# A four-batch decoder layer on one core: more stages in halves, two batches of masks spread by TensorE, memsets later, a new hand-written order

## The reference, cut to what matters

```
x = x + attn(layernorm(x))            # softmax(-gamma * |yi - yj|^2) @ y, 512 x 512 a batch
x = x + xattn(layernorm(x), ctx)      # q, k, v, 16 heads; scores = q.k/sqrt(8) + slope*(i-j)
x = x + ffn(layernorm(x))             # 8 experts, the 2 with the largest logits are summed

logits = einsum('bsh,eh->bse', hidden_states, router_w) + router_b
_, top_k_indices = top_k(softmax(logits), 2)
mask = one_hot(top_k_indices, E).sum(axis=-2)
out = einsum('bse,ehd,bsd->bsh', mask, expert_w, hidden_states) + einsum('bse,eh->bsh', mask, expert_b)
```

## Time and profile before

| | |
|---|---|
| median of 3 runs | 208.95 us (208.78 to 220.65) |
| the profiled execution, device time | 208.65 us |
| its span | 206.9 us |
| PE, share of the span with a matmul | 91% |
| DVE | 70% |
| ACT | 50% |
| POOL | 35% |
| mean granted TensorE clock | 0.984 of full speed |

### The profile page before, as it was taken

One profiled execution on the slowest core, in us unless ns is written; L12 is line 12 of the kernel. 1 busy time (PEld: TensorE's weight loads), 2 busy tenths in 40 slices (PEclk: granted clock), 3 DMA queues, 4 the chain that ended last, 5 costly groups with the idle time before them and its releaser, 6 DMA issues. The chain is left out here.

```text
span 206.9 us, 4043 instructions
## 1 busy us (share of the span) xinstructions
PE 188.4 (91%) x1418; PEld 119.8 (58%) x1427; DVE 144.2 (70%) x395; ACT 104.1 (50%) x204; POOL 72.3 (35%) x122
## 2 busy tenths in 40 slices
PE   7999999998999999799988876799998999698894
PEld 2454589744475432546585456753397854398674
DVE  2844969799999999195249999787188712736662
ACT  2037989739625888799850300178613638400100
POOL 6986014166500000024504289205906000793000
PEclk9999999999999999999999999999999789979999
DMA  4910073582710000640479047023000024000002
GB/s 126 355 15 2 21 196 113 153 194 91 187 46 21 0 0 12 175 121 3 143 141 302 22 154 150 22 73 133 28 36 0 8 82 182 0 0 3 2 0 101
DMA packets 12972, 17.66 MB, mean 85 GB/s; under 512 B 1332, under 2 KB 10548, under 8 KB 12256
## 3 DMA queue, kind: packets, MB, share of 16 engines
q1 hardware_dynamic: 12952, 17.41, 29.4%
HBM read 11.02 MB, written 6.38 MB: 84 GB/s over the span
## 5 line engine op out<-in xcount | busy, mean ns | idle before, releaser
L1103 DVE TENSOR_REDUCE nm<-bank 128x3 f32<-128x462 f32 (+1 forms) x88 | 48.3, 612 | 5.3 <-PE bank L1337 5.0
L926 ACT ACTIVATE pt<-bank 128x512 f32<-128x512 f32 x80 | 41.9, 615 | 8.7 <-PE bank L1375 8.1
L1472 PE MATMUL bank<-ewT,ym 128*128 128x128 f32 x256 | 35.1, 291 | 0.0
L1472 PEld LDWEIGHTS bank<-ewT,ym 128*128 128x128 f32 x256 | 32.7, 205 | 0.8 <-issue 0.6
L813 POOL TENSOR_TENSOR ym<-mask_all,y3T 128x512 f32<-128x512 bf16 x24 | 27.2, 1168 | 13.4 <-DMA mask_all<-e_scratch 13.4
L1337 PE MATMUL bank<-ks,qs 99*128 99x308 bf16 (+1 forms) x171 | 26.0, 263 | 1.3 <-DVE nm L1103 1.2
L796 POOL TENSOR_SCALAR ve<-mv 128x4 f32<-128x4 f32 (+1 forms) x5 | 1.0, 196 | 67.8 <-DVE mv L987 67.8
L1337 PEld LDWEIGHTS bank<-ks,qs 99*128 99x128 bf16 x171 | 13.4, 98 | 15.2 <-DVE nm L1103 6.2
L1375 PE MATMUL bank<-qs,ks 105*128 105x512 bf16 (+1 forms) x80 | 20.6, 342 | 0.6 <-DMA qs<-m_scratch 0.6
L1214 PE MATMUL bank<-idle 128*128 128x512 bf16 x60 | 16.4, 426 | 1.7 <-DVE idle L978 1.5
L1404 PE MATMUL bank<-pt,vm 128*32 128x512 f32 (+1 forms) x160 | 17.7, 518 | 0.0
(11 more groups left out here) (143 smaller groups left out, 271.4 us busy)
## 6 DMA issues: line engine op xcount, KB each, us to landing
mask_all<-e_scratch SPq DMA_DIRECT2D x3, 1024.0 KB, 5.0
ks<-k_scratch SPq DMA_DIRECT2D x4, 480.0 KB, 4.2
q_scratch<-qpart SPq DMA_DIRECT2D x3, 384.0 KB, 2.5
qs<-q_scratch SPq DMA_DIRECT2D x3, 384.0 KB, 4.8
xs<-in_x_dram SPq DMA_DIRECT2D x4, 256.0 KB, 4.0
k_scratch<-mask_all SPq DMA_DIRECT2D x4, 240.0 KB, 2.4
q_scratch<-qpart SPq DMA_DIRECT2D x3, 256.0 KB, 2.1
qs<-q_scratch SPq DMA_DIRECT2D x3, 256.0 KB, 5.3
```

What stands on the lines that cost most here:

```text
L926: nc.scalar.activation(pt[:, n % RING, :], at("scores", b, i)[:, :], ACT.Exp).then_inc(exps, 1)
L1103: v.tensor_reduce(nm[b][:, n:n + heads], at("maxima", b, g)[:, 0:heads * J].rearrange("p (s j) -> p s j", s=heads), AX.X, ALU.max, negate= ...
L1472: last = mm(at("experts", b, p)[:, tile(t)], ym[:, e, tile(t)], ewT[:, e, :], start=False, stop=(e == E - 1), skip_group_check=True)
```

## The change

The configuration, and what the table of dummy matmuls becomes:

```diff
-PARTS2 = (2, 1, 1, 1)
-PARTS3 = (1, 1, 1, 2)
+PARTS2 = (2, 2, 2, 2)
+PARTS3 = (1, 1, 2, 2)
...
-SPREAD = (3,)
+SPREAD = (2, 3)
...
 WARM = {
-    "y1T:0.0": 43, "kp:0.0": 2, "sqT:0.0": 1, "maxima:1.0": 3, "divide:0.1": 2, "aoT:0.0": 1, "maxima:2.0": 9,
-    "y2T:3.0": 2, "route:1.0": 1, "y3T:3.0": 1, "spread:3.0": 1,
+    "y1T:0.0": 28, "sqT:0.0": 4, "probs:1.1": 3, "maxima:0.0": 5, "y2T:3.0": 22, "query:3.0": 2,
+    "maxima:2.0": 1,
 }
```

All five texts of `ORDER` and the eight of `TURNS` are rewritten. One line of POOL's and one of DVE's:

```diff
     "gpsimd": """
-        weights:0.0 setup:0.0 gamma:0.0 zeros:0.0 rstd1:0.0 rstd1:1.0 squares:0.0 bias:0.0 y1g:1.0 squares:1.0
+        setup:0.0 gamma:0.0 rstd1:0.0 squares:0.0 bias:0.0 rstd1:1.0 squares:1.0 y1g:1.0 zeros:0.0 weights:0.0
...
     "vector": """
...
+        y2:0.0 key_values:0.1 rowmax:1.0 key_values:0.2 key_values:0.3 gather:0.1 split:0.0 y1:2.0 y2:0.1
+        keys:0.1 gather:1.0 split:0.1 dist:2.0 dist:2.1 y2:1.0 gather:1.1 y1:3.0 dist:2.2 dist:2.3 y2:1.1
```

```diff
-        q_out = [[sem(f"q_out{i}_{k}") for k in range(3 * PARTS2[i])] for i in range(B)]
+        q_out = [[sem(f"q_out{i}_{k}") for k in range(3 * max(PARTS2[i::2]))] for i in range(2)] * 2
...
-                pool.wait_ge(gamma_ready, 2)
...
-                pool.wait_ge(rstd1_ready, g_ + 1)
-
             def squares(g_, _):
 
                 m = members(g_)
+                pool.wait_ge(rstd1_ready, g_ + 1)
+                pool.wait_ge(gamma_ready, 2)
...
-                    act.wait_ge(e_in, ONE * b)
+                    act.wait_ge(e_in, ONE * sum(i not in SPREAD for i in range(b)))
...
             def select(b, k):
-                p, e = k // (E // 2), k % (E // 2) * 2
+                per = PARTS3[b]
+                p, e = k * per // E, k * per % E
...
-                dve.wait_ge(spread_ps, k + 1)
+                dve.wait_ge(spread_ps, E * SPREAD.index(b) + k + 1)
```

More of the change, by code:

```diff
@@ L141 @@
-        values:1.2 scores:1.19 self:3.0 values:1.3 values:1.4 mask:0.0 divide:1.0 divide:1.1 self:3.1 probs:3.2
-        aoT:1.0 wo:1.0 probs:3.3 self:3.2 self:3.3 maxima:2.0 maxima:2.1 maxima:2.2 maxima:2.3 maxima:2.4
-        maxima:2.5 maxima:2.6 y2T:3.0 maxima:2.7 y3T:1.0 maxima:2.8 maxima:2.9 query:3.0 maxima:2.10
-        maxima:2.11 maxima:2.12 maxima:2.13 maxima:2.14 maxima:2.15 maxima:2.16 maxima:2.17 experts:0.0
-        maxima:2.18 maxima:2.19 maxima:2.20 maxima:2.21 route:1.0 experts:0.1 experts:0.2 experts:0.3 mT:2.0
@@ L161 @@
-        spread:3.5 spread:3.6 experts:3.8 spread:3.7 experts:3.9 experts:3.10 experts:3.11 experts:3.12
-        experts:3.13 experts:3.14 experts:3.15
+        start:0.0 y1T:0.0 sqT:0.0 dist:0.0 dist:0.1 dist:0.2 keys:0.0 dist:0.3 y1T:1.0 keys:0.1 sqT:1.0
+        key_values:0.0 sqT:2.0 probs:0.0 dist:1.0 probs:0.1 self:0.0 probs:0.2 self:0.1 dist:1.1 dist:1.2
+        dist:1.3 probs:0.3 self:0.2 y2T:0.0 self:0.3 query:0.0 probs:1.0 probs:1.1 self:1.0 y1T:2.0 probs:1.2
+        y2T:0.1 sqT:3.0 query:0.1 self:1.1 dist:2.0 probs:1.3 dist:2.1 self:1.2 self:1.3 dist:2.2 y2T:1.0
@@ new lines @@
+        self:3.0 values:0.4 divide:0.0 scores:1.0 scores:1.1 divide:0.1 scores:1.2 probs:3.3 scores:1.3
+        scores:1.4 aoT:0.0 scores:1.5 self:3.1 scores:1.6 wo:0.0 scores:1.7 scores:1.8 scores:1.9 scores:1.10
+        scores:1.11 values:1.0 scores:1.12 scores:1.13 scores:1.14 values:1.1 scores:1.15 scores:1.16
+        scores:1.17 scores:1.18 values:1.2 values:1.3 y2T:2.0 scores:1.19 divide:1.0 query:2.0 values:1.4
+        y2T:2.1 y3T:0.0 divide:1.1 query:2.1 route:0.0 aoT:1.0 self:3.2 wo:1.0 self:3.3 mask:0.0 y2T:3.0
@@ new lines @@
+    """,
+    """
+        dist:0.1 sqT:2.0 query:0.1 y2T:1.0 y1T:3.0 maxima:0.7 probs:2.0 probs:2.1 maxima:0.19 maxima:1.2
+        maxima:1.6 maxima:1.11 scores:0.2 maxima:1.17 scores:0.9 scores:0.12 scores:0.16 self:3.0 maxima:2.2
+        maxima:2.8 maxima:2.14 maxima:2.20 maxima:3.1 pv:2.0 scores:2.11 scores:2.14 scores:2.17 maxima:3.18
+        experts:1.0 experts:2.0 experts:3.1
+    """,
+    """
+        dist:0.2 dist:1.0 y2T:0.0 self:1.0 dist:2.3 maxima:0.9 dist:3.1 maxima:0.21 maxima:1.4 maxima:1.9
+        probs:3.2 scores:0.1 maxima:1.16 scores:0.8 scores:0.11 mT:1.0 pv:0.1 scores:1.2 scores:1.5 scores:1.9
+        scores:1.13 scores:1.18 y3T:0.0 mask:0.0 y2T:3.1 maxima:2.6 maxima:2.13 mask:1.0 scores:2.3 scores:2.7
+        maxima:3.9 divide:2.0 maxima:3.19 scores:3.0 mT:3.1 pv:3.0 scores:3.11 scores:3.14 spread:2.1
+        spread:2.3 experts:2.1
@@ new lines @@
+    """,
+    """
+        kp:0.0 probs:0.0 probs:0.2 dist:1.3 self:1.1 maxima:0.2 query:1.1 maxima:0.12 maxima:0.17 maxima:1.0
+        self:2.1 y2T:2.0 divide:1.1 y2T:3.0 maxima:2.4 maxima:2.10 maxima:2.15 maxima:2.21 maxima:3.2
+        maxima:3.5 pv:2.1 maxima:3.14 maxima:3.17 maxima:3.20 wo:2.0 scores:3.5 wo:2.1 divide:3.0 pv:3.2
+        divide:3.3 spread:2.6 mask:3.0 experts:3.0
+    """,
+    """
+        dist:0.3 self:0.1 probs:1.2 dist:2.2 y2T:1.1 maxima:0.8 maxima:0.14 dist:3.2 probs:2.3 maxima:1.5
+        maxima:1.10 maxima:1.14 scores:0.5 maxima:1.19 pv:0.0 divide:0.1 aoT:0.0 scores:1.7 pv:1.0 y2T:2.1
+        wo:1.0 maxima:2.1 maxima:2.7 experts:0.0 scores:2.4 maxima:3.6 maxima:3.10 scores:2.12 pv:2.2
+        divide:2.2 scores:3.6 y3T:2.0 scores:3.12 route:2.1 scores:3.18 spread:2.2 wo:3.0 spread:2.7 spread:3.1
+        spread:3.6
@@ L216 @@
+    """,
+    """
+        y1T:1.0 probs:0.1 dist:1.1 query:0.0 y2T:0.1 dist:2.1 maxima:0.3 dist:3.0 maxima:0.16 self:2.0
+        scores:1.16 divide:1.0 route:0.0 query:3.0 maxima:2.5 route:1.0 maxima:2.17 scores:2.1 maxima:3.3
+        maxima:3.7 scores:2.10 scores:2.13 scores:2.15 pv:2.3 scores:3.4 pv:3.1 divide:3.1 scores:3.17 mask:2.1
+        aoT:3.1 y3T:3.0 spread:3.0 spread:3.4
     """,
```

265 lines of the change are left out of this document (127 added, 138 removed).

## The result

The changed kernel takes 201.62 us in the median of 4 executions (201.13 to 202.76), the kernel before 208.87 beside it: a ratio of 0.9664, 95% interval 0.9613 to 0.9716. It is faster by 3.4%. The forecast was 203.7 with a range of 199.5 to 209.5.

A forecast was written before the change was run, and what follows sets the result against it. TensorE and VectorE were taken to bound alternate stages, neither the end. Start to batch 1's residual -3.6, batch 2's seam -1.4, PE's extra work +2.6, end -2.8 sum to -5.2 us: 203.7 forecast, range 199.5 to 209.5.

The forecast's parts named there:

- The start: Up to the first distance tile: later memsets and 15 fewer dummies bring it 4.4 us earlier, first maxima 3.1 earlier.
- The blocked casts: At the first keys' cut: memsets on POOL hold up DVE's casts, taken as 0.5 us, bounds nothing to 3.6.
- my signs of being wrong: Included first maxima from 48 us, key casts over 0.6 us, batch 2's second-half scores later than 34 us behind the residual.
- Halves of the queries: Queries of batches 1 to 3 halved, three more DMAs each way a batch: no effect taken, 1.5 us at worst.
- Batch 2 in halves: From batch 1's residual to batch 2's scores: first half at 25.1 us, second about 34, net 1.4 us gained.
- scores 5.8 later: Batch 2's first scores follow the transposition of its first maxima by 5.8 us, from 19.3 to 25.1 behind the residual.
- Routing 2.4: DVE's routing between batch 2's first cut and its remaining groups of maxima takes 2.4 us.
- No gap of 3 us for mcat: Sign of being right: PE no longer stands about 3 us (3.18 before) waiting for batch 2's cut of maxima.
- What PE pays and the end: Spread matmuls and halved values cost PE 2.5 to 2.8 us; at the end 2.8 us of idle go.
- The rival of the full clock: Both half-clock stretches in the last two stages vanish with PE's idle: 200.3 us, chance 0.14.
- the eaten head start: Rival: DVE's full list before the first maxima swallows the early start, -3.6 becomes at most -1.2: 206.3 us, chance 0.24.
- the ping-pong: Rival: at the end DVE's selects and PE's experts wait on each other, eight turns give 212 us; chance 0.17.

The follow-up runs named there:

- the clock held: Changed kernel with 12 more dummies ahead of the transposition of batch 2's first maxima: 201.63 us, ratio 0.9661 to the kernel before.
- the tightened start: Changed kernel with large memsets in GpSimd's gap before gamma, small ones later, and 23 dummies instead of 28 ahead of the transpositions: 200.92 us, ratio 0.9651.
- the late routing: Changed kernel with VectorE's routing of batch 1 behind batch 2's second cut, TensorE's route and mask moved to match: 213.06 us, ratio 1.0134.

## Why the prediction was right, and where it was not

**The start.** Right, by its own steps: y is written by 8.1, the transpositions begin when the 28 dummies end, at 9.52, the distance tile follows 2.0 us later (I had 1.8), and the head start of 4.65 us becomes 2.6 at the first maxima (I had 3.1) and 4.2 at the residual (3.6). Putting 15 dummies back moved all of it by 3.3 and the time by 3.0. Both parts are needed: with the memsets ahead of the root 1.8 us are lost again.

**The blocked casts.** I took 0.5 us for memsets against casts. One cast took 1.87 us beside the memsets of vm and vt and 0.48 without them, so the term was 1.4. This was one of my signs of being wrong, a cast over 0.6 us, and it came true. It cost nothing, because DVE waits for PE right behind the keys: the list that I called full is not full there. From distance tile to first maxima the kernel now takes 2.1 us more than before, where I had 1.3; since a faster cut of the keys didn't shorten it, the 0.8 us are in another part of the chain, and which one stays open.

**Halves of the queries.** I took nothing, and looked only at what the added DMAs might cost. With whole batches the first maxima of batch 2 come 10.7 us behind the residual instead of 8.5. The step left out that a half query is at the DMAs earlier, and that it is batch 2 that waits for it.

**Batch 2 in halves.** This step failed, though one of its terms was right: the cut beside the selects took 4.1 us as said (4.0), and the transposition of the first maxima came 19.2 us behind the residual (19.3). Two others were wrong. The first is "scores 5.8 later", which I had taken from batch 0, where the maxima's way through DRAM decides. The scores of batch 2 came 9.5 us behind their transposition, and TensorE did not wait in between: in its list five experts of batch 0 (40 matmuls) and groups of maxima stand ahead of them. With the clock held it is still 7.9 us, in the tightened start 8.1. That is why the first scores came at 28.7 and not at 25.1.

The second is the routing. I went on with "Routing 2.4", its duration where it stands alone, although the same selects still run. It took 4.75 us:
```profile
122.04 1.22 DVE L1182 TENSOR_TENSOR cmp_eq<-lg 128x256 f32<-128x256 f32 x1
123.18 1.38 DVE L1183 TENSOR_TENSOR cmp_gt<-lg 128x256 f32<-128x256 f32 x1
124.59 1.28 DVE L1185 COPY_PREDICATED cmp_gt<-earlier,cmp_eq 128x256 f32<-128x256 uint32 x1
```
against 0.42, 0.42 and 0.45 us in the run with the late routing. "No gap of 3 us for mcat" held by the letter only: TensorE stood 2.76 us, and 3.25 in the runs with 43 dummies and with the tightened start. The second half's scores came 38.2 us behind the residual instead of 34, another of my signs of being wrong. Of the 4.2 us, 1.8 are the long fall of the clock in this execution (36.4 with the clock held). The other 2.4 are there in every trace of this order: with the clock held the second cut ends 29.7 us behind the residual where I had 28.1, and the scores follow it by 6.7 instead of 5.9. That the longer routing is behind most of it is argued from DVE's list; the one run that shortened it moved other work too. Taking off the 2.7 us of work that, by the prediction's count, TensorE then had in hand, the seam lost 2.7 where I had counted a gain of 1.4.

**What PE pays and the end.** From the tenth score to the last expert it is 64.5 us before and 57.3 after, 7.2 less. By the prediction's own counts 2.7 are the work done ahead, and 3.4 the halved clock of the two stretches of 3.4 us, where this kernel has full clock; no run measures either by itself. About 1.0 is left for the spread's price and the end's gain together, where I had 0.2 (2.6 paid, 2.8 gained). PE's idle time behind the last values fell by 2.1 us to 3.2, just short of "under 3". So the net is about right and its smallness misleads: in the new order the spread of batch 2 is worth 7.8 us.

**The sum.** In the trace the residual came 0.6 us earlier than forecast, the seam of batch 2 took 4.2 more, and what follows took 4.4 less, of which by my estimate 3.4 is the clock, whose halves I had left in. They moved, from the last two stages, which TensorE bounds, to one where 3.4 us of them cost nothing and 10.2 us cost 1.8. The forecast's reasons held up to 105 us; behind it two errors of about 4 us cancelled, and that the total came out so close is luck. The rival of the full clock (200.3) was half true, the ones of the eaten head start and of the ping-pong weren't: y3 of batch 3, 2.30 us blocked, takes 0.57 now, and DVE's 16 selects wait for TensorE's spread twice in all, 2.3 us together.
